# Turning the projection rows of a decoder layer with transposing transfers instead of TensorE

## The reference

```python
x = x + _L0_attn_ref(_layernorm(x, axis=-1), ln_gamma, ln_beta, q_gamma, k_gamma, w_q, w_k, w_v, w_o, b_o)

def _L0_attn_ref(x, ...):
    xn = _layernorm(x, ln_gamma, ln_beta)        # per row of 512
    q, k, v = proj(w_q), proj(w_k), proj(w_v)    # xn @ w.T, 8 heads of 64
    qn = _rmsnorm(q, q_gamma) * dh ** (-0.5)
    kn = _rmsnorm(k, k_gamma)
    attn = softmax(qn @ kn.T)
    return concat(attn @ v) @ w_o.T + b_o
```

## Time and profile before

| | |
|---|---|
| median of 3 runs | 2325.62 us (2323.33 to 2331.7) |
| the profiled execution | 2321.48 us, its span 2319.6 us |
| granted TensorE clock, mean | 0.982 of full speed |
| busy share PE, DVE, ACT, POOL | 94%, 67%, 69%, 64% |
| first phase, batch 0 | first projection matmul at 19.30 us, last one done at about 167 us |
| first phase, batch 1 | last one done at about 1319 us |

### The profile page before, as it was taken

How to read it: one execution, slowest core, us unless ns; L and a number is a source line. 1 busy time by engine, 2 the same in 40 slices (tenths; PEclk the granted TensorE clock), 3 DMA queues, 4 the chain that set the end, 5 groups by cost and what they waited for, 6 DMA issues and landing times. The chain is left out here.

```text
span 2319.6 us, 63272 instructions
## 1 busy us (share of the span) xinstructions
PE 2189.6 (94%) x22392; PEld 1256.9 (54%) x22392; DVE 1565.5 (67%) x2601; ACT 1609.7 (69%) x1831; POOL 1483.9 (64%) x980
## 2 busy tenths in 40 slices
PE   6998999999997989899999899999999978998999
PEld 3544666666665445444445446666666644554444
DVE  6987777777776756753379877777777766667532
ACT  4555999999998556731145579999999975566210
POOL 4324998989988577731233158898998976867210
PEclk9998999999999999999999989999999999999999
DMA  4210000000001301102122100000000022011000
GB/s 105 64 37 5 2 9 9 9 9 9 9 0 29 105 1 38 46 15 77 46 55 58 34 1 10 0 9 9 9 9 9 4 63 67 1 47 37 19 22 34
DMA packets 102338, 65.10 MB, mean 28 GB/s; under 512 B 75346, under 2 KB 75346, under 8 KB 102226
## 3 DMA queue, kind: packets, MB, share of 16 engines
q1 hardware_dynamic: 102226, 63.57, 12.3%
HBM read 46.69 MB, written 8.39 MB: 24 GB/s over the span
## 5 line engine op out<-in xcount | busy, mean ns | idle before, releaser
L751 POOL TENSOR_TENSOR probs_l<-wide 128x1024 f16<-128x1024 f32 x448 | 986.3, 2234 | 162.3 <-PE bank L803 120.7
L887 DVE TENSOR_REDUCE pm<-bank 128x1 f32<-128x512 f32 x1024 | 680.5, 688 | 249.1 <-PE bank L759 244.2
L878 ACT ACTIVATE wide<-bank,shift 128x1024 f32<-128x1024 f32 x512 | 570.4, 1114 | 37.3 <-DVE probs_l L901 30.7
L870 ACT ACTIVATE wide<-bank,shift 128x1024 f16<-128x1024 f32 x512 | 567.6, 1109 | 10.9 <-PE bank L775 10.9
L759 PE MATMUL bank<-ko,q_hh 128*128 (+1 forms) x1024 | 397.0, 390 | 22.3 <-PEq L454 12.2
L774 PE MATMUL bank<-q_hh,ko 128*128 (+1 forms) x1024 | 389.9, 381 | 18.1 <-ACT wide L878 13.1
L775 PE MATMUL bank<-q_lm,k_h 65*128 (+1 forms) x1024 | 389.8, 381 | 0.0
L788 PEld LDWEIGHTS bank<-v_hl,wide 128*128 128x128 f16 x4096 | 287.5, 98 | 63.4 <-issue 5.7
L788 PE MATMUL bank<-v_hl,wide 128*128 (+1 forms) x4096 | 319.8, 192 | 0.1
L790 PE MATMUL bank<-v_hl,wide 128*128 (+1 forms) x4096 | 318.0, 193 | 0.0
L790 PEld LDWEIGHTS bank<-v_hl,wide 128*128 128x128 f16 x4096 | 267.4, 96 | 58.7
(11 more groups left out here) (211 smaller groups left out, 4187.5 us busy)
## 6 DMA issues: line engine op xcount, KB each, us to landing
wide<-in_x SPq DMA_DIRECT2D x32, 256.0 KB, 2.6
q_lm<-in_x SPq DMA_DIRECT2D x32, 256.0 KB, 3.2
ko<-in_L_ffn_W SPq DMA_DIRECT2D x32, 256.0 KB, 3.8
q_hh<-q_hh SPq DMA_DIRECT2D x32, 128.0 KB, 2.6
ko<-k_h SPq DMA_DIRECT2D x32, 128.0 KB, 2.8
out<-bo_b SPq DMA_DIRECT2D x16, 256.0 KB, 2.0
out<-xbo_b SPq DMA_DIRECT2D x16, 256.0 KB, 2.0
q_lm<-nm SPq DMA_DIRECT2D x248, 0.2 KB, 4.9
```

Of the source, the lines that this page charges most:

```text
L751: pool.tensor_tensor(probs_l[:, p % 2, :], probs[:, p % 2, :], probs_h[:, p % 4, :], ALU.subtract).then_inc(pl_pool, 1)
L870: act.activation(probs_h[:, p % 4, :], SB[p % 2][:, :], ACT.Exp, bias=shift[:, 0:1]).then_inc(ph_ready, 1)
L878: act.activation(probs[:, p % 2, :], SB[p % 2][:, :], ACT.Exp, bias=shift[:, 0:1]).then_inc(p_ready, 1)
L887: dve.tensor_reduce(pm[:, s, k:k + 1], MB[k % 2], AX_X, ALU.max).then_inc(mx_free, 1)
```

## The change

Tiles 0 and 1 are handled as before. For tiles 2 to 15:

- the rows are normalised on POOL instead of DVE;
- ACT makes the high part from the rows as they are (before they are turned), at the end of `step(t)` for tile t+2, after the high part of v; POOL subtracts to make the low part. Both lie in the part of `v_hl` that tile t+2's v will fill later;
- SP issues two transposing transfers (`turn`), one for the high and one for the low part, 128 x 512 fp16 each, SBUF to SBUF, into slot `s` of `rows_h` and `rows_l`. `turn(t+2)` stands at the start of SP's iteration t, ahead of the wait for tile t's heads, so behind the load of tile t+5. It waits for the low part of t+2 (`a_tl`) and for the v projection of tile t (`a_v_done`), which is the last reader of the slot;
- PE, before the q projection of tile t, waits for `a_turned`, that is until both transfers have landed. Its row transposes, ACT's and DVE's reads of their bank go away;
- POOL's `ones` comes after tile 2's low part;
- the loop over tiles is written out instead of a hardware loop.

```diff
-        def row_normalise(dve, b, t, s, first=False):
+        def row_normalise(eng, b, t, s, first=False):
...
+                eng.wait_ge(a_t_done, 2 * b + min(t - 1, 2))
+                if t >= 4:
+                    eng.wait_ge(a_tl, b * (KB - 2) + t - 3)
...
+        def turn(t):
+            sp.wait_ge(a_tl, b * (KB - 2) + t - 1)
+            sp.wait_ge(a_v_done, T0 + t - 1)
+            sp.nop(nofuse=True)
+            for src, dst in zip(as_rows(t), (rows_h, rows_l)):
+                sp.dma_start_transpose(dst[:, t % 2, :].rearrange("p (g r) -> p g r", g=DC), src)\
+                    .then_inc(a_turned[t % 2], 16)
+
         for t in range(KB):
+            if t + 2 < KB:
+                turn(t + 2)
...
 # POOL
             if next2:
                 row_scale(pool, b, t + 2, s)
+                row_normalise(pool, b, t + 2, s)
                 row_affine(pool, b, t + 2, s)
+                high, low = as_rows(t + 2)
+                pool.wait_ge(a_th, b * (KB - 2) + t + 1)
+                pool.tensor_tensor(low, rows_n[:, s, :], high, ALU.subtract).then_inc(a_tl, 1)
...
 # PE
-            pe.wait_ge(a_xl, T0 + t + 1)
+            if t < 2:
+                pe.wait_ge(a_xl, 2 * b + t + 1)
+            else:
+                pe.wait_ge(a_turned[s], turned(t))
...
-            if next1:
+            if not before:
                 row_transposes(pe, b, t + 1, 1 - s)
...
 # ACT
-            if next1:
+            if not before:
                 row_high(act, b, t + 1, 1 - s)
...
+            if next2:
+                act.wait_ge(a_xn, T0 + t + 3)
+                act.activation(as_rows(t + 2)[0], rows_n[:, s, :], ACT.Copy).then_inc(a_th, 1)
...
 # DVE
-            if next1:
+            if not before:
                 row_low(dve, b, t + 1, 1 - s)
-            if next2:
-                row_normalise(dve, b, t + 2, s)
```

More of the change, by code:

```diff
@@ L206, in decoder_layer @@
         a_xl = sem("a_xl")
+        a_th = sem("a_th")
+        a_tl = sem("a_tl")
+        a_turned = [sem(f"a_turned{i}") for i in range(2)]
         a_q_done = sem("a_q_done")
@@ L335, in row_scale @@
                 .then_inc(a_rs, 1)
-        def row_normalise(dve, b, t, s, first=False):
+        def row_normalise(eng, b, t, s, first=False):
             T0 = b * KB
-            dve.wait_ge(a_rs, T0 + t + 1)
+            eng.wait_ge(a_rs, T0 + t + 1)
             if not first:
-                dve.wait_ge(a_t_done, T0 + t - 1)
-            dve.tensor_scalar(rows_n[:, s, :], rows_in[:, s, :], rows_mv[:, s, 0:1], rows_rs[:, 1, s:s + 1],
+                eng.wait_ge(a_t_done, 2 * b + min(t - 1, 2))
+                if t >= 4:
+                    eng.wait_ge(a_tl, b * (KB - 2) + t - 3)
+            eng.tensor_scalar(rows_n[:, s, :], rows_in[:, s, :], rows_mv[:, s, 0:1], rows_rs[:, 1, s:s + 1],
                               ALU.subtract, ALU.mult).then_inc(a_y, 1)
@@ L359, in row_transposes @@
             if not first:
-                pe.wait_ge(a_xl, T0 + t)
+                pe.wait_ge(a_xl, 2 * b + t)
             for d in range(DC):
@@ L366, in row_high @@
         def row_high(act, b, t, s):
-            act.wait_ge(a_t_done, b * KB + t + 1)
+            act.wait_ge(a_t_done, 2 * b + t + 1)
             act.activation(rows_h[:, s, :], banks[2][:, :], ACT.Copy).then_inc(a_xh, 1)
         def row_low(dve, b, t, s):
-            dve.wait_ge(a_xh, b * KB + t + 1)
+            dve.wait_ge(a_xh, 2 * b + t + 1)
             dve.tensor_tensor(rows_l[:, s, :], banks[2][:, :], rows_h[:, s, :], ALU.subtract).then_inc(a_xl, 1)
@@ L474, in decoder_layer, with over_tiles, as_rows, turned @@
                     T0 = b * KB
[L476 to L486, removed]
+                    def over_tiles(step):
+                        for t in range(KB):
+                            step(t, t % 2, t > 0, t + 1 < KB, t + 2 < KB)
+                    def as_rows(t):
+                        r = v_hl[:, t * (H * VW):t * (H * VW) + 2 * D].rearrange("p (s n) -> p s n", s=2)
+                        return r[:, 0, :], r[:, 1, :]
+                    def turned(t):
+                        return (b * (KB // 2 - 1) + t // 2) * 32
                     @block.sync
@@ L513, in ones @@
                         def ones():
-                            pool.wait_ge(a_xn, T0 + 3)
+                            pool.wait_ge(a_tl, b * (KB - 2) + 1)
                             pool.nop(nofuse=True)
@@ L523, in step @@
                                 row_scale(pool, b, t + 2, s)
+                                row_normalise(pool, b, t + 2, s)
                                 row_affine(pool, b, t + 2, s)
+                                high, low = as_rows(t + 2)
+                                pool.wait_ge(a_th, b * (KB - 2) + t + 1)
+                                pool.tensor_tensor(low, rows_n[:, s, :], high, ALU.subtract).then_inc(a_tl, 1)
                             if not before:
                                 ones()
-                        over_tiles(pool, step)
+                        over_tiles(step)
                     @block.tensor
@@ L565, in step @@
                             project(s, "v", VB, a_v_done)
-                        over_tiles(pe, step)
+                        over_tiles(step)
                         head_transposes(KB - 1)
@@ L606, in step @@
                                            scale=INV_WS).then_inc(a_vh, 1)
+                            if next2:
+                                act.wait_ge(a_xn, T0 + t + 3)
+                                act.activation(as_rows(t + 2)[0], rows_n[:, s, :], ACT.Copy).then_inc(a_th, 1)
                         act.preload_act_table(ACT.Sqrt)
                         split_high(act, b, PIECES_P1[2:], stage1, wh)
-                        over_tiles(act, step)
+                        over_tiles(step)
                         heads_high(KB - 1)
@@ L672, in _ @@
                         split_low(dve, b, PIECES_P1[2:], stage1, wh, wl)
-                        over_tiles(dve, step)
+                        over_tiles(step)
                         heads_low(KB - 1)
```

## The result

The changed kernel takes 2400.4 us (median of 4 runs, 2396.4 to 2403.5), the kernel before 2324.7: a ratio of 1.031, interval 1.029 to 1.033, 76 us slower. The forecast was 2376 with 2335 to 2462 as its range. The profiled execution has a span of 2401.4 us, 81.8 over before's 2319.6.

The account below looks back on a forecast made before the run. PE was taken to bound the first phase at 9.08 us a tile. Per batch, 32.2 us of stalls less 8.3 saved plus 1.3 of clock, over two batches, gave +50.4 us: median 2376 us, range 2335 to 2462.

Parts of the forecast that it names:

- The stall total: PE's waits for turned rows in the first phase: 11.65 plus 5 x 4.1, 32.2 us per batch.
- PE is the bound in mid-phase: First phase: PE busy 9.08 of 9.08 us per tile, DVE 8.46; after the change 8.64 against 7.2.
- The saving of 8.3 us per batch: First phase: PE loses the row transposes of tiles 2 to 15 and a 1.80 us pause behind POOL.
- When the turn is issued: SP's queue: the turn stands behind a load awaiting the next tile's normalise, so transfers start 7.25 us after E(n-2).
- E(n-2): The moment the last projection matmul of tile n-2 is done, from which the prediction times the turn.
- T, the two transfers: Time for both transposing transfers to land: 5.5 us taken, 2.6 to 10.4 kept; over 1.4 stalls PE.
- signs of being wrong: Turn issued right after the low part, landing under 1 or over 7 us, or issue holding SP much beyond 0.6.
- the first rival: The two transposing transfers run one after the other, T = 10.4 us: 2460 us; chance 0.24, including nearly so.
- The stalls: PE before the q projection: 11.65 us at tile 2, 4.1 at tiles 4, 6, 8, 10, 12, none from 13.
- The clock: PE's clock falls after a long pause: 1.3 us, counted once per batch, for tile 2 only.
- Transfers in a row: Rival: transposing transfers do not overlap, starving PE harder, 67 us per batch, 2460 us; chance 0.24, including nearly so.
- Faster, because SP's wait is not the last: Rival listed second: an earlier normalise lets the turn go at 2.95 us, hiding the transfers; 2313 us (-0.55%), chance 0.07.

Follow-up runs that it names:

- experiments 1: Changed kernel with SP issuing the turn of tile t+3 ahead of the load of tile t+6, and tile 2's ahead of tile 5's load: 2328.7 us.
- experiment 9: Changed kernel with DVE taking the statistics of tile t+3 before v's low part of tile t, SP's order kept: 2353.6 us.
- experiment 5: Changed kernel with the turn issued ahead of the load and POOL's row of ones set after the last tile: 2312.8 us, ratio 0.9939.
- experiment 2: Changed kernel with PE's waits before tiles 2, 4, 6, 8, 10 and 12 filled by unread transposes of the identity: 2378.6 us.
- Experiment 6: The kernel before, without any turn, with only POOL's row of ones moved after the last tile: 2329.1 us, ratio 1.001.
- experiment 7: Changed kernel with tiles 2 to 15 normalised on DVE right after their statistics instead of on POOL: 2375.9 us, ratio 1.022.
- experiment 4: Changed kernel with plain copies of the same bytes in place of the transposing transfers, rows left unturned: 2387.0 us, ratio 1.025.

## Why the prediction was right

The mechanism was the one forecast, and experiments 1 and 9 show it from its two ends: the turn was late because SP's order puts a load ahead of it, that load waits for the next tile's normalise, and its statistics hang on the end of the last v projection. Move the turn, and 72 us go; move the statistics, and 47 go. The stall total also came out nearly as worked out, but that is luck: two errors of opposite sign, 1.6 us in the turn's issue and 1.65 us in the transfers, cancel.

- **PE is the bound in mid-phase, DVE close behind.** Right. With the waits gone (experiment 5), PE is busy 20.00 of 20.00 us with a tile of 8.64 us, and from its first projection to the end of tile 15 batch 0 takes 141.1 us (21.0 to 162.1) against 147.7 before (19.3 to 167.0). The saving of 8.3 us per batch, less tile 2's 1.4, is there to 0.3 us.
- **When the turn is issued.** Forecast 7.25 us after E(n-2), measured 8.82 (92.12 against 83.30). POOL's normalise takes 2.07 us, not the 1.27 of a tensor-tensor operation of the same size, 0.8 of it. I took the nearest row by engine and size, but the operation is another one, with two operations and a scalar for each partition. The other 0.7 is DVE's small `rp` instruction, 1.00 us instead of 0.17. At tile 2 it is the same: turn at 45.86, forecast 43.9.
- **T, the two transfers.** Forecast 5.5, measured 3.85 us (92.12 to 95.97). The trace of the changed kernel has each issue at 1.26 us on SP, double a copy's 0.63, and the landing 2.6 us after its own issue:

```profile
wide<-v_hl SPq DMA_TRANSPOSE x28, 2.6
```

  (28 in batch 0.) 1.26 + 2.6 = 3.86. The nearest row was the plain copy of the earlier trace rows for the landing, not the scattered one. The prediction had an issue of much more than 0.6 us among its signs of being wrong, and this one came true; it would have shown in the time, had the landing not been 2.3 us shorter than assumed. The Trainium skill (Advanced Engine Details and Errata, X-Bar Transpose) has transposing DMAs as fast as regular ones: the landing agrees, 2.6 against 2.6 to 2.8 us, but the issue on SP takes twice as long. By the figure of the Trainium skill for one 128 x 128 block of bf16 (VectorE: DVE Perf Modes, The three transpose paths), eight blocks would be an estimated 10.5 us; the eight of fp16 here took 3.85. (10.5 us is the time of the first rival, not of the second as the prediction has it.)
- **The stalls.** For tile 6, 8.82 + 3.85 - 8.64 = 4.0 us; seen 3.9; forecast 4.1. Tile 2: 11.6, forecast 11.65. Per batch 31.1 against 32.2. The places, every second tile from 4 to 12 and none from 13 on, were as worked out.
- **The clock: the term that was too small.** Forecast one fall of 1.3 us per batch; there were six of 2.5 us. In batch 0 the phase grew by 37.6 us (185.3, from 19.6 to 204.9, against 147.7): 31.1 of waits less 8.3 saved leaves 14.8, that is 2.5 for each of six pauses. Experiment 2 shows the same 2.5 by itself. Two errors: the 3.9 us pause, between the known 2.73 and 6.10, I counted at none; and the price I took from the kernel's start, where 7 matmuls ran at half speed, while here it was all 12 of the q projection (8 of them at tile 4, where the first four still ran at full speed). That price was also rounded up: 2.46 less 1.29 is 1.2 us, not 1.3. Here is the stretch around tile 6's start, whose clock is 0.50, or 1.2 GHz, and that before tile 4, where PE still idles at 1.00:

```profile
96.00:101.00 5.00, 5.00 (x12) 1.71 (x13) 0.74 (x2) 0.00 (x0) 3.93 (x5) 0.50 0.25 52
...
68.00:73.00 5.00, 1.11 (x6) 0.35 (x5) 4.84 (x10) 2.79 (x5) 4.10 (x4) 1.00 0.46 105
```

  This term accounts for the distance between the forecast and the result: (14.8 - 1.3) x 2 = 27 us, less 2 for the stalls, against 24 missing.
- **The rivals.** Transfers in a row: they overlap, as the landing row says. Faster, because SP's wait is not the last: 2313 us was its price, and experiment 5, where that wait is made not to be the last, measures 2312.8. Its saving of 8.3 less a wait of 1.9 at tile 2 is also near what the trace of batch 0 has, 8.3 less 1.4. It failed here because nothing shortened the chain through the statistics by the 4 us it needed. That the two times agree to 0.2 us is partly chance, as the next point shows.
- **The rest of the kernel.** The two first phases account for 37.6 + 37.1 of the 81.8 us. The rest of the work is 3.1 us longer after batch 0's phase and 3.7 after batch 1's. It is the same work at a slightly lower clock, as the stretches behind batch 0's phase show, first in the changed kernel, then in the one before (columns as in the earlier trace rows):

```profile
205.00:1209.00 1004.00, 952.19 (x10441) 553.09 (x10440) 653.05 (x1074) 721.44 (x773) 687.37 (x429) 0.97 0.12 25
167.00:1168.00 1001.00, 949.30 (x10441) 551.92 (x10440) 652.18 (x1074) 721.23 (x773) 688.76 (x429) 0.98 0.11 25
```

  In experiment 5 this counts for more. Its profiled execution has a span of 2314.5 us, only 5.1 under before's, though its two phases are 6.6 and 8.9 us shorter: the work ahead of the first phase is 1.7 us longer, that behind the phases 3.6 and 5.0. Its gain of 14 us is that of the medians. Why the clock of the rest differs between executions stays open.

## What to carry to other kernels

Before an instruction is put on a queue that nobody has waited for so far, list what stands ahead of it there: a prefetch that waits for a freed buffer is harmless as the last of a queue and expensive as the first. Here the edit costs 3%, and the same edit with two lines of SP's queue swapped and a memset moved gains 0.6%. Price a wait on TensorE with the clock that it costs as well: a pause of 3.9 us cost 6.4.

## What the runs showed of the hardware

- **A small DVE instruction waits for POOL's.** `rp` (128 x 16 float32) takes 0.17 us in the mid-phase of the kernel before. In the changed one it takes 1.00 us on even tiles, and ends at 85.95, when POOL's subtraction (84.77 to 85.92) has just ended; on odd tiles it takes 0.31 and ends at 94.35, POOL's addition at 94.32. Where nothing runs on POOL it is 0.16 (experiment 9, 91.99, POOL done at 91.96). Others, such as v's low part, kept their time next to POOL's. Experiment 6 separates it: with nothing changed but the place of POOL's memset, the `rp` beside it goes from 0.17 to 5.14 us and ends within 0.04 us of the memset. The Trainium skill (SBUF — State Buffer, SBUF: two separate sides) has GpSimd and some DVE instructions share a pair of ports, those in a two-port mode or, against a GpSimd instruction that reads SBUF, with two SBUF inputs; whoever starts first keeps the pair for its whole instruction. The durations agree; that `rp` runs in such a mode no run here shows.
- **Which pauses cost clock.** Pauses of 1.3 to 1.9 us left it at 1.00 in experiments 2, 5, 7 and 9, and pauses of 3.3 us and more were followed by a fall each time. Between them the length alone does not decide. In the kernel before, 2.09 us (batch 1, to 1192.25) were followed by 0.66 over 5 us; in experiment 2, 2.32 us were followed by 0.66 and 2.42 us by 1.00; in experiment 7, 2.69 us by 0.68 (70 to 75 us); in experiment 4, 3.18 us by 1.00 (tile 4) and 3.18 us by 0.72 (tile 12). The 2.73 us at the end of batch 0's phase, which the prediction took as harmless, were followed by 1.00 in the kernel before, but by 0.50 in the changed kernel, whose eight head transposes take 1.97 us there and not 1.25. What else matters no run here tells.
- **A transposing transfer** of 128 x 512 fp16 within SBUF holds SP for 1.26 us and lands 2.6 us after its issue (medians of 56), against 0.60 and 2.5 us for the plain copy of experiment 4.
